# The lane's one-hots of the sort held as 32-bit words in place of 16-bit ones

## The reference

```python
h = jnp.maximum(_layernorm(x, axis=-1), 0.0)
# layer 0: for each edge relu(concat(h[src], h[dst]) @ W0.T + b0), summed into the row of src
m_ij = jax.nn.relu(x_ij @ W.T + b)
x = x + jax.ops.segment_sum(m_ij, src, num_segments=1250)
h = jnp.maximum(_layernorm(x, axis=-1), 0.0)
# layer 1: (h @ W1.T)[src] * edge_weight, summed into the row of dst, then a leaky relu with alpha
msgs = (h @ W.T)[row] * edge_weight[:, None]
out = jax.ops.segment_sum(msgs, col, num_segments=1250)
x = x + jnp.where(out >= 0, out, alpha * out)
```

## Time and profile before

| what | value |
|---|---|
| median of 3 runs | 994.15 us (994.05 to 995.83) |
| the profiled execution | 996.06 us, span 994.3 us |
| busy PE, DVE, ACT, POOL | 958.2, 875.8, 768.6, 650.9 us |
| mean granted TensorE clock | 0.996 of full speed |
| the sort's columns | from 41.5 us (first `hot_tile`) to 251.3 us (last placement) |
| the join of the table, L707 | starts at 252.58 us |

### The profile page before, as it was taken

One profiled execution on the slowest core, in us unless ns is written; L12 is line 12 of the kernel. 1 busy time (PEld: TensorE's weight loads), 2 busy tenths in 40 slices (PEclk: granted clock), 3 DMA queues, 4 the chain that ended last, 5 costly groups with the idle time before them and its releaser, 6 DMA issues.

```text
span 994.3 us, 20364 instructions
## 1 busy us (share of the span) xinstructions
PE 958.2 (96%) x4761; PEld 778.4 (78%) x4762; DVE 875.8 (88%) x1778; ACT 768.6 (77%) x1651; POOL 650.9 (65%) x942
## 2 busy tenths in 40 slices
PE   5889999999899999999999999999999999999997
PEld 5777888878688877888888887888887788777776
DVE  7899999988499999999999999999999788874444
ACT  3689999989588888888888888888889766655110
POOL 4788788887677777777777777777777655530000
PEclk9999999999999999999999999999999999999999
DMA  4300000000211111111111111111111010010011
GB/s 145 87 2 4 3 3 4 2 3 2 65 43 43 41 41 42 41 41 41 42 42 43 43 41 41 42 43 42 42 43 34 30 33 32 21 44 1 21 42 42
DMA packets 35732, 35.16 MB, mean 35 GB/s; under 512 B 7650, under 2 KB 31967, under 8 KB 35684
## 3 DMA queue, kind: packets, MB, share of 16 engines
q1 hardware_dynamic: 30394, 31.45, 10.2%
q0 software_dynamic: 4368, 0.68, 1.7%
q10 hardware_dynamic: 922, 2.44, 0.7%
HBM read 30.92 MB, written 3.28 MB: 34 GB/s over the span
## 4 chain that ended last, share of the span: by engine, by line
PE 70%; DVE 2%; ACT 1%; issue 1%; POOL 0%; POOLq 0%
PE node_ps L1216 8%; PE edge_ps L1255 8%; PE edge_ps L1260 8%; PE edge_ps L1261 8%; PE node_ps L1217 8%; PE edge_ps L1256 8%; PE m_ps L1227 4%; PE psum L1368 3%; PE psum L1370 3%; PE psum L1369 3%; PE m_ps L1350 1%; PE edge_ps L1328 1%; PE edge_ps L1329 1%; PE edge_ps L1320 1%; PE edge_ps L1324 1%; PE edge_ps L1321 1%
## 5 line engine op out<-in xcount | busy, mean ns | idle before, releaser
L1457 ACT ACTIVATE msg_hi<-edge_ps 128x512 fp32r<-128x512 f32 x332 | 197.7, 595 | 58.4 <-PE edge_ps L1261 58.4
L1172 POOL TENSOR_TENSOR M<-M,pair_w 125x125 f32 x332 | 160.7, 484 | 124.5 <-DVE pair_w L1604 94.7
L1618 DVE SCALAR_TENSOR_TENSOR msg_lo<-edge_ps,msg_hi 128x512 fp32r<-128x512 f32 x332 | 223.7, 683 | 15.4 <-ACT msg_hi L1457 10.8
L444 POOL DMA_INDIRECT edge_table<-fields,row_no x132 | 165.9, 1257 | 44.5 <-issue 44.5
L907 ACT ACTIVATE lane_piece<-hot_lane,fields 125x128 fp32r<-125x128 bf16 x528 | 163.0, 396 | 4.4 <-DVE hot_lane L547 4.4
L755 PE MATMUL psum<-hot_tile,lane_piece 125*128 125x384 f32 x594 | 145.5, 365 | 7.5 <-ACT lane_piece L907 5.4
L1156 POOL TENSOR_TENSOR hot_w<-hot_d,weight_l 128x252 fp32r<-128x252 bf16 x166 | 141.1, 850 | 0.0
L1216 PE MATMUL node_ps<-msg_hi,hot_s 128*125 128x512 f32 x332 | 134.6, 405 | 0.0
L1255 PE MATMUL edge_ps<-b_hi,turned_d 125*128 x332 | 131.8, 397 | 1.1 <-issue 0.8
L1260 PE MATMUL edge_ps<-a_hi,turned_s 125*128 x332 | 131.3, 395 | 0.7 <-ACT turned_s L1441 0.7
L1256 PE MATMUL edge_ps<-b_lo,turned_d 125*128 x332 | 130.9, 394 | 0.0
(11 more groups left out here) (264 smaller groups left out, 2051.6 us busy)
## 6 DMA issues: line engine op xcount, KB each, us to landing
spread<-edge_rows SPq DMA_DIRECT2D x190, 125.0 KB
out_dram<-result SPq DMA_DIRECT2D x10, 224.0 KB
edge_table<-fields,row_no POOLq DMA_INDIRECT x132, 2.6
w_in<-in_L_gnn_W_dram ACTq DMA_DIRECT2D x1, 2048.0 KB, 12.1
S<-in_x_dram SPq DMA_DIRECT2D x1, 1792.0 KB
w_in<-in_L_gnn_W_dram SPq DMA_DIRECT2D x1, 1024.0 KB, 5.6
S<-in_x_dram SPq DMA_DIRECT2D x1, 448.0 KB
edge_table<-zeros POOLq DMA_DIRECT2D x1, 384.0 KB, 8.9
```

Of the source, the lines that this page charges most:

```text
L444: pool.indirect_dma_start(table_dram[:, :], bass.IndirectOffsetOnAxis(ap=row_no[:, c:c + 1], axis=0), fields[:, c, 0:TABLE_FIELDS], None). ...
L1457: act.activation(msg_hi[j][:], edge_ps[j][:], ACT.Relu).then_inc(hi_ready, 1)
L1618: dve.scalar_tensor_tensor(out=msg_lo[j][:], in0=edge_ps[j][:], scalar=0.0, in1=msg_hi[j][:].bitcast(F32), op0=ALU.max, op1=ALU.subtract). ...
```

## The change

One declaration changes. The six buffers of `hot_lane` become 32-bit floating point; the instruction that writes them and those that read them stay as they are and take the type from the tile. The buffers take 1536 bytes more in each row of the on-chip memory, and those allocated behind them in the first block move up by that. The order of the instructions on every engine is the same before and after.

```diff
@@ -195,7 +195,7 @@
             hot_tile = [sb1(f"hot_tile{k}", [EROWS, NT], F32R) for k in range(RING)]
             lane_piece = [sb1(f"lane_piece{k}", [EROWS, PIECES, TILE], F32R) for k in range(RING)]
-            hot_lane = [sb1(f"hot_lane{k}", [EROWS, TILE], BF16) for k in range(RING)]
+            hot_lane = [sb1(f"hot_lane{k}", [EROWS, TILE], F32) for k in range(RING)]
             fields = sb1("fields", [EROWS, ECOLS, FIELDS], F32)
```

## The result

| | median | lowest to highest | runs |
|---|---|---|---|
| before | 994.15 us | 993.58 to 995.83 | 5 |
| after | 1005.43 us | 1002.93 to 1008.24 | 5 |

The kernel with 32-bit lanes is slower: ratio 1.0102, interval [1.0084, 1.0120]. The forecast was 997.0 us with a range up to 1000.2; the sign came true, the size did not: 11.3 us in place of 2.9.

The account below looks back on a forecast made before the run. VectorE's own work was taken to bound the sort's first four chunks. 4.7 us, less 0.8, plus 0.3, made placing 4.2 us late; 1.3 hidden left 2.9: 998.96 us profiled, 997.0 at the median, range 993.2 to 1000.2.

Parts of the forecast that it names:

- the lane's 33 ns: Writer L547 on VectorE: storing four bytes instead of two lengthens each 128-element operation by 33 ns, 243 to 276 ns.
- the readers at nothing: The 528 ScalarE activations that read the lanes: reading four bytes instead of two costs nothing.
- the 1.3 us that the load hides: End of the sort: placing may end 1.3 us late at no cost, since L707 waits for the table's load.
- L707 released by TensorE: VectorE's first step after the sort: the last placement, no longer the table's load, ends its wait, 2.9 us later.
- the fillers just off the path: TensorE's 18 fillers behind placing end 4.2 us later, with 0.2 us left before the next block's first product.
- 143 × 33 ns: VectorE's lane operations up to the end of chunk four: 4.7 us added, with no gap to hide them.
- the first rival: VectorE's waits for GpSimd soak up 2.9 of the 4.7 us; time 994.2 us; chance 0.27.
- Over many columns the waits should stay what they are on average: Argument against soaking up: a later VectorE also meets more GpSimd instructions per chunk, so its waits stay unchanged on average.
- 4.2 us of lateness at the end of placing: TensorE's placing at the sort's end: ends 4.2 us later, at about 255.5 us.
- The second rival: GpSimd's 132 indirect DMAs are each held up 33 ns, the table's load 4.4 us late; 998.5 us; chance 0.08.
- The margin of 8.9 us: Last chunk's slots, written at 207.74 us, to its first DMA at 216.62: a 4.5 us shift fits, load unmoved.
- The third rival: Mixed widths push L547 to one element a step, 104 ns more each; 8.6 us, 1002.8 us; chance 0.07.

Follow-up runs that it names:

- The two repeats with 32-bit lanes: Kernel after with, ahead of GpSimd's indirect DMAs, four waits for a semaphore long reached (1008.06 us), or a one-element memset in the first four chunks (1006.21 us).

## Why the prediction was wrong

Right, by its own steps: the lane's 33 ns (31 measured); the readers at nothing; no idle time on VectorE up to 217 us; the 1.3 us that the load hides; L707 released by TensorE; the fillers just off the path (L1279 starts at 262.71, 5.73 us later than before, as L707 does by 5.67).

The term 143 × 33 ns was of the right kind: 3.5 us between starts where 4.7 stood.

The step that failed is the sentence under the first rival, "Over many columns the waits should stay what they are on average". It took VectorE's waits for GpSimd to be a random draw, unmoved by 33 ns, and so put their change at nothing. In the copy columns both engines run at a fixed pace, each wait puts VectorE at the same place against the next DMA, and whether that place is caught is decided by an edge at 0.51 us. In the rows shown it lay at 0.49 us before and at 0.53 to 0.54 after. The tile waits of the copy columns went from 5.1 us to 15.1. In the steps of the tile operations that is +10.3 us there, −2.8 elsewhere, and the +7.5 is what the sum lacked: 4.2 us of lateness at the end of placing became 6.9 in the profiled pair, and would have become 9.7 with the start of before, if nothing else had moved.

The rows to see it were there: a wait that "ends at GpSimd's own time" gives the next start, and one more column's length the next. I read single waits and did not follow one into its successor. The Trainium skill, "SBUF — State Buffer", section Who interferes with whom, has the first of the two hold the shared ports for its whole instruction. Here the measurement differs: by the table above a tile operation that starts in the first 0.51 us of GpSimd's DMA is free (caught in 1 of 63 before), and one that starts from there to 0.90 us is mostly caught (44 of 61), until past the DMA's end. The prediction had seen that only a part blocks, and used it against the rival. But a part is enough for a lock.

The first rival was half right. Outside the copy columns the tile operations did give back 2.8 us of waits. The lanes' waits, on which it was built, were no cushion at all: their excess over the median fell from 5.1 us to 1.8, and VectorE won nothing by it, since behind the 25 lengthened lanes of before the next instruction starts no later than behind the others (0.16 us after the lane's start at the median). The 288 ns that the prediction gives as the lanes' mean belong to all 176; its rows 2 have 278 for the stretch that it argues on.

The second rival was there too, at 3.2 of its 4.4 us, on the DMAs. That the last DMA still ended near 248 us (248.66), as forecast, was luck: the DMAs began 2.72 us sooner with everything else. The margin of 8.9 us between the last chunk's slots and its first DMA, of which the prediction spent 4.5, shrank to 0.42 us (215.42 to 215.84). The load would not have decided in after even so, since placing was later still. The third rival did not come, the lane ran at the quicker rate; it gave 1002.8 us, near the measured time, for a reason that is not there.

Left open: where the spread of after comes from (5.3 us over five runs, 2.3 in before). Of the 11.3 us at the median the profiled pair shows 6.9, 5.7 of them up to L707; the other 4.4 are the distances of the two profiled executions from their medians (+1.91 and −2.50). The two repeats with 32-bit lanes, whose L707 is 12.4 and 7.6 us late, show that the sort's end alone moves by such amounts. The start of the columns against GpSimd's DMAs hardly differs (the first DMA comes 0.88 to 0.99 us after the first tile operation in every kernel of this order); whether a tenth of a microsecond there matters was not tried.

## What to carry to other kernels

Where two engines with fixed periods shut each other out, follow one wait to its end and add the length of the loop: if the next start falls into the shut part again, the loop takes the other engine's period. Here 31 ns decided it. Price a small edit there by how far that start is from the edge, not by count times duration. And before shortening the loop, look at who is later once it is free: here it was the other engine's own chain.

## What the runs showed of the hardware

- Only a part of GpSimd's indirect DMA of 1.18 us shuts out VectorE's tile operation: a start under 0.51 us was caught in 1 of 63 cases, from 0.51 to 0.90 in 44 of 61, and those that waited over 0.3 us ended at a median of 1.34 us (after) and 1.36 us (before) behind the DMA's start. GpSimd pays as well: its DMAs last 1257 ns on average before and 1281 after.
- A lane operation lengthened from 0.24 to 0.42 us or more did not delay the start of the VectorE instruction behind it (0.16 us from start to start behind the lane at 71.76 before).
- Two GpSimd memsets of one element between two DMAs cost 12 ns of period, one costs nothing, and four 70 ns.
- A 16-bit lane of 256 elements and a 32-bit one of 128 take the same 273 to 274 ns.
